# Two 64x64 projections as four array tiles, and a stage's loop written out

## The reference

```
left  = (a @ left_proj_w.T  + b) * sigmoid(a @ left_gate_w.T  + b)     (times a mask)
right = (a @ right_proj_w.T + b) * sigmoid(a @ right_gate_w.T + b)     (times a mask)
t     = einsum('bikc,bjkc->bijc', left, right)
t     = layernorm(t)
x2    = x + (t @ out_proj_w.T + out_proj_b) * sigmoid(a @ gating_w.T + gating_b)
p     = softmax(layernorm(x2) @ router_w + router_b)    over 8 experts
out   = x2 + sum over the 2 best experts of p_e / (p_1 + p_2) * (layernorm(x2) @ expert_w[e] + expert_b[e])
```

## Time and profile before

| what | us |
|---|---|
| median of three runs (lowest, highest) | 1189.2 (1185.09, 1192.96) |
| the profiled execution | 1189.99 |
| its span, first to last instruction | 1188.0 |
| PE busy in the span | 1080.7 |
| DVE | 882.2 |
| POOL | 747.6 |
| ACT | 598.8 |

### The profile page before, as it was taken

The page is one execution under the profiler, slowest core; times in us unless marked ns, Lnnn a source line. Parts: engine busy times, 40 slices in busy tenths (PEclk is TensorE's granted clock), DMA queues, the critical chain, the costliest instruction groups (busy, mean ns, idle before and its releaser), DMA issues.

```text
span 1188.0 us, 21300 instructions
## 1 busy us (share of the span) xinstructions
PE 1080.7 (91%) x5402; PEld 594.6 (50%) x5402; DVE 882.2 (74%) x3030; ACT 598.8 (50%) x1070; POOL 747.6 (63%) x728
## 2 busy tenths in 40 slices
PE   1788989889786599999999999999999999999987
PEld 1566666678674344444444444444444444454432
DVE  3999999611115768888888888887888788888872
ACT  0455666411111245666566556565656565656552
POOL 5777888121222357777777767776767776777632
PEclk9899999899887879999999999999999999999986
DMA  7388679967770101111111111111111111111100
GB/s 194 115 268 284 229 274 293 328 198 235 209 234 27 30 19 51 46 45 42 50 47 44 36 54 40 49 45 45 36 53 36 54 36 53 36 54 36 36 27 27
DMA packets 98895, 119.15 MB, mean 100 GB/s; under 512 B 6390, under 2 KB 72182, under 8 KB 96758
## 3 DMA queue, kind: packets, MB, share of 16 engines
q1 hardware_dynamic: 97138, 117.74, 30.9%
q10 hardware_dynamic: 1668, 0.46, 0.2%
HBM read 67.33 MB, written 50.33 MB: 99 GB/s over the span
## 4 chain that ended last, share of the span: by engine, by line
PE 75%; DVE 14%; issue 5%; DMA 2%; ACTq 1%; POOL 1%; ACT 1%; SPq 1%; DVEq 0%; POOLq 0%
PE b_m L807 22%; PE ring L793 9%; PE ein L710 7%; DVE stage L889 6%; PE b_d L754 6%; PE b_g L746 6%; PE b_t L747 5%; PE pr_a L672 4%; PE b_m L801 3%; DVE bst L876 3%; PE b_g L741 3%; PE b_g L735 3%; PE ring L815 3%; PE b_t L735 2%; PE ring L822 1%
## 5 line engine op out<-in xcount | busy, mean ns | idle before, releaser
L451 POOL TENSOR_TENSOR zb<-bcs,x2d 128x512 f32<-128x512 f32 x224 | 285.7, 1275 | 234.8 <-ACT bcs L588 233.6
L807 PE MATMUL b_m<-zb,w_exp 128*64 128x512 f32 x1024 | 284.7, 636 | 0.1
L1052 DVE TENSOR_TENSOR zb<-ring,x2d 128x512 f32<-128x512 f32 x288 | 197.5, 686 | 90.9 <-PE ring L793 90.2
L588 ACT ACTIVATE bcs<-ring 128x512 f32<-128x512 f32 x224 | 133.9, 598 | 245.5 <-PE ring L793 245.2
L572 ACT ACTIVATE x2d<-x2t 64x512 f32<-64x512 f32 x256 | 160.5, 627 | 3.4
L672 PE MATMUL pr_a<-w_proj,xts 64*128 64x256 f32 x1024 | 138.3, 399 | 22.1 <-DVE stage L889 21.4
L889 DVE SCALAR_TENSOR_TENSOR stage<-pr_a,mt,sig_a 128x128 f32<-128x128 f32 x512 | 147.8, 418 | 9.4 <-ACT sig_a L521 9.4
L793 PEld LDWEIGHTS ring<-wt,sel 32*128 32x128 f32 x512 | 49.4, 186 | 177.6 <-DVE zb L1052 83.1
L793 PE MATMUL ring<-wt,sel 32*128 32x512 f32 x512 | 131.0, 504 | 5.2 <-DVE zb L1052 4.4
L672 PEld LDWEIGHTS pr_a<-w_proj,xts 64*128 64x128 f32 x1024 | 95.1, 189 | 51.0 <-issue 30.9
L521 ACT ACTIVATE sig_a<-pr_a 128x512 f32<-128x512 f32 x128 | 76.4, 597 | 78.9 <-PE pr_a L672 78.9
(11 more groups left out here) (133 smaller groups left out, 1820.7 us busy)
## 6 DMA issues: line engine op xcount, KB each, us to landing
left_right_scratch<-stage SPq DMA_DIRECT2D x16, 2048.0 KB, 7.5
chunk<-left_right_scratch SPq DMA_DIRECT2D x24, 1024.0 KB, 9.0
xc<-in_x SPq DMA_DIRECT2D x64, 256.0 KB, 2.7
out<-outc SPq DMA_DIRECT2D x64, 256.0 KB, 2.0
chunk<-left_right_scratch SPq DMA_DIRECT2D x12, 384.0 KB, 7.5
chunk<-left_right_scratch SPq DMA_DIRECT2D x8, 192.0 KB, 4.9
chunk<-left_right_scratch SPq DMA_DIRECT2D x4, 256.0 KB, 8.0
chunk<-left_right_scratch SPq DMA_DIRECT2D x8, 64.0 KB, 4.7
```

The lines of the kernel that those rows point to most:

```text
L451: pool.tensor_tensor(zb[:, m % NZ, :], bcs[:, tiles_before(POOL_TILES, ku, ku, m) % 2, :], x2d[:, ku % 2, m % 2, :], ALU.mult)\
L588: act.activation(bcs[:, tiles_before(POOL_TILES, ku, ku, m) % 2, :], ring[:, bcast_bank(ku % 2, m), :], ACT.Copy).then_inc(bcast_out, 1)
L807: ins = pe.matmul(b_m[t * C:(t + 1) * C, :], w_exp[:, ep, :], zb[:, (2 * ep + t) % NZ, :], start=False, stop=ep == EP - 1, skip_group_chec ...
L1052: dve.tensor_tensor(zb[:, m % NZ, :], ring[:, bcast_bank(ku % 2, m), :], x2d[:, ku % 2, m % 2, :], ALU.mult)\
```

## The change

out_gate issues four matmuls of 64 rows by 64 columns. Tile (t, t) of the array, rows and columns of half t, multiplies the half t of xtn and writes the half t of b_g. Tile (t, 1 - t) multiplies the half t of ttn and writes the other half of b_t. So that each token's output lands in its own half, ScalarE's copy puts the upper half of b_t into the lower half of ttn and the other way round, in two copies of 64 partitions. The weights need no zeros: w_og is [128, 2, 64], and its memset goes. The semaphores g_ready and og_ready are raised by the last matmul of each kind.

The loops of all five engines in the last stage are written out: each slot is issued with its own number u, while ku, by which buffers are chosen, runs from 0 to 11 again and again.

```diff
-        w_og = keep("w_og", [P, 2, P])
+        w_og = keep("w_og", [P, 2, C])
...
-            pool.memset(w_og[:, :, :], 0.0).then_inc(pool_const, 1)
...
-                act.activation(ttn[:, :], b_t[:, :], ACT.Copy).then_inc(turns_out, 1)
+                for half in range(2):
+                    ins = act.activation(ttn[half * C:(half + 1) * C, :], b_t[(1 - half) * C:(2 - half) * C, :], ACT.Copy)
+                ins.then_inc(turns_out, 1)
...
             def out_gate(v):
                 pe.wait_ge(turns_out, v + 1)
-                pe.matmul(b_g[:, :], w_og[:, 0, :], xtn[:, :], start=True, stop=True).then_inc(g_ready, 1)
-                pe.matmul(b_t[:, :], w_og[:, 1, :], ttn[:, :], start=True, stop=True).then_inc(og_ready, 1)
+                half = [slice(t * C, t * C + C) for t in range(2)]
+                for t in range(2):
+                    g = pe.matmul(b_g[half[t], :], w_og[half[t], 0, :], xtn[half[t], :], start=True, stop=True)
+                    o = pe.matmul(b_t[half[1 - t], :], w_og[half[t], 1, :], ttn[half[t], :], start=True, stop=True)
+                g.then_inc(g_ready, 1)
+                o.then_inc(og_ready, 1)
...
-            for u in range(-4, 2 * HEAD):
-                slot(u, u)
-            with pe.Fori(0, LOOPS) as i:
-                for k in range(2 * HEAD, 2 * (HEAD + CYCLE)):
-                    slot(i * (2 * CYCLE) + k, k)
-            for u in range(2 * TAIL, UNITS + 1):
-                slot(u, u)
+            for u in range(-4, UNITS + 1):
+                slot(u, u % (2 * CYCLE) if u >= 0 else u)
...
-            dve.wait_ge(pool_const, 5)
+            dve.wait_ge(pool_const, 4)
...
-                    dve.tensor_copy(w_og[part, w, part], w_proj[part, (4 + w) * C:(5 + w) * C])
+                    dve.tensor_copy(w_og[part, w, :], w_proj[part, (4 + w) * C:(5 + w) * C])
```

More of the change, by code:

```diff
@@ L39 @@
 CYCLE = 6
-HEAD = 4
-LOOPS = (STEPS - 2 * HEAD) // CYCLE
-TAIL = HEAD + LOOPS * CYCLE
 TOK = STEP_J
@@ L313, in _ @@
                 load_unit(v, v)
-            for u in range(XC - 6, 2 * HEAD):
-                slot(u, u)
-            with sp.Fori(0, LOOPS) as i:
-                for k in range(2 * HEAD, 2 * (HEAD + CYCLE)):
-                    slot(i * (2 * CYCLE) + k, k)
-            for u in range(2 * TAIL, UNITS + 1):
-                slot(u, u)
+            for u in range(XC - 6, UNITS + 1):
+                slot(u, u % (2 * CYCLE) if u >= 0 else u)
             for h in range(2):
@@ L482, in _ @@
             ins.then_inc(sel_made, 1)
[L483 to L489, removed]
+            for u in range(-3, UNITS):
+                slot(u, u % (2 * CYCLE) if u >= 0 else u)
         @block.scalar
```

## The result

The changed kernel takes 1149.4 us (median of three runs, 1146.6 to 1158.81) where the one before takes 1189.2: a ratio of 0.9685, with a 95% interval of 0.9642 to 0.9727. A second set of runs gave 1146.42 against 1190.38: 0.9641 (0.9613 to 0.967). The forecast was 1151.5, in a range of 1138 to 1178. Ratios are of the mean times of the fast executions; the one slow execution, 1191.6 us of the loop alone, is left out, and since that kernel's profile is of it, only its full pipe, at clock 1.00, is compared.

A forecast was written before the change was run, and what follows sets the result against it. The prediction took PE (TensorE) to bound the last stage. From the profiled 1190.0 us it took 7.1 for the loop and 32.2 for the projections and added 0.8 for the fill: 1151.5 us, range 1138 to 1178.

The forecast's parts named there:

- The loop, 7.1 us: Last stage: three jumps back, each with the slot behind it costing 2.36 us, vanish when written out; 7.1 us saved.
- out_gate and the turns, 2.36 to 1.60: PE's projections and following turns: four tiles overlap in 1.01 us, turns take 0.59; 0.76 us saved a slot.
- The odd slot keeps 0.33, the even one 0.76: Full pipe: ScalarE's gate sigmoid limits odd slots' saving to 0.33 us; even slots keep all 0.76; 32.2 us over 59 units.
- PE's share of the stage was to fall to about 95%: Last stage: PE's busy share down from 99% to about 95%, a sign expected in the profile after.
- ScalarE's copy, 0.5 to 0.63 us later, covered except in the fill: ScalarE's added ttn copy raises turns_out 0.5 to 0.63 us later, delaying PE only in the fill's four units.
- The fill, +0.8: Fill: four units each pay 0.5 us for the copy and win back about 0.3; 0.8 us added.
- The drain, 0: Work left after the last unit's out_gate starts: the forecast sum gave it no term.
- What came before the stage, 0: Very start of the kernel: w_og's memset goes where PE is not the bound; 0 us.
- partial overlap: Rival on out_gate: passes start in staggered pairs, 1164.2 us, or ScalarE's run slips, 1169; chance 0.18.
- two groups one behind the other: Rival on out_gate: g and g, o and o cannot run together; 1190 us, no change; chance 0.08.
- rival 3: out_gate's passes start in program order, four tiles taking 2.30 us; slower, 1215 us; chance 0.05.
- Fetching the long code: Rival on the written-out loops: code fetching stops engines as the jump did, 7.1 us stay; 1158.6 us; chance 0.11.

The follow-up runs named there:

- e1: The kernel before with its five engines' loops written out, projections as before; 1187.14 us against 1192.25, ratio 0.9945.

## Why the prediction was right

Step by step, by the full pipe's 58 periods:

- *The loop, 7.1 us.* 7.0 in the first profile of before, 8.4 in the second, where the clock fell at a jump. Right, with two small terms that were put at nothing and nearly cancel: 0.5 for entering the loop, and 0.6 for the even slots, a little longer when written out. That no stop comes back: right (PE busy 682.50 of 682.50).
- *out_gate and the turns, 2.36 to 1.60.* The four tiles and the turns behind took 1.02 + 0.59 = 1.61 in even slots, and 0.75 was saved wherever nothing else was late. Right, and taken from the two nearest rows.
- *The odd slot keeps 0.33, the even one 0.76.* Measured 11.97 - 11.63 = 0.34 and 11.56 - 10.82 = 0.74. The cause named, ScalarE's sigmoid behind its run of copies, is shown by moving it. That tile 6 stands right behind it was in the prediction too, and is shown by the version that moves both. Of the 0.4 us that PE was to wait for the sigmoid at x_turn, it waits 0.17 at the turns for tile 6 and 0.23 at x_turn for the sigmoid. PE's share of the stage was to fall to about 95%, and is 98.8% (643.14 of 651.00): waits of 0.4 us in 29 slots are 1.8% of the stage, so that number didn't follow from the prediction's own. Both steps together: e1's 682.4 less 651.1 is 31.3 us, against 32.2 for 59 units.
- *ScalarE's copy, 0.5 to 0.63 us later, covered except in the fill.* Covered in the full pipe, yes: without it the periods are the same. Its size was under-read: ttn is done 1.81 us after xtn's start (1046.63 to 1048.44), where it was 1.08 before (1103.37 to 1104.45 in an odd slot), so 0.73. ttn's two halves start 0.61 us apart (1047.24 and 1047.85), where a copy of 128 partitions starts 0.49 behind the one ahead of it.
- *The fill, +0.8.* Measured 56.9 against 59.2. The sign is wrong, and the number is the difference of larger ones: the second and third unit took 9.64 us each instead of 6.86, the fourth and fifth 15.95 and 10.72 instead of 21.41 and 13.11.
- *The drain, 0.* Measured -7.9 and -5.5 us against the two profiles of before. This term was missing. The drain's length goes with the time that TensorE spends at the half level in it (29.0 and 24.6 us before, 8.6 after), as the last section shows; what sets that time is open.
- *What came before the stage, 0.* The first out_gate started at 386.9 us, against 381.7 and 384.5 before: 5.2 and 2.4 later. Of the 5.2, 0.7 is the second copy, as above. The rest lies ahead of the stage: the einsum's last pass ended at 373.6 us, against 369.2 and 371.9 before, two profiles of one kernel that are 2.7 apart, and 370.7 in the version without the swap, which has no memset either.

So the forecast of 1151.5 is right in its large terms, 39.3 foreseen and 38.3 measured for the full pipe. The profiled execution, 1146.6, is 4.9 below it: 1.0 less saved in the pipe and 5.2 more in front, against 3.1 less in the fill and 7.9 less in the drain. That the median came out within some 2 us of the forecast is luck: these terms cancel in part, and the median of the three lies 2.8 above the profiled one.

Of the rivals: partial overlap, and two groups one behind the other, fall with the eight starts above; the second is exactly what the version without the swap does (2.46 us, 1187). Program order, as rival 3 had it, falls with the same starts: out_gate takes 1.02 us and not 2.30. The trace has no order of the instructions other than their starts, so whether the passes also stand in the stream in that order is not shown, for these tiles as for L807's halves; the prediction's word that the trace disagrees there was too strong. Fetching the long code falls with the loop alone. The rule of the Trainium skill (TensorEngine Tiling (Array Packing), Restrictions and Gotchas) that different row tiles cannot access one PSUM bank at the same time did not show: the two L731 passes of different rows write b_g together, at 1050.07 and 1050.08, in different partitions. Whether it holds for the same partitions of one bank was not tried. The four at once, and the piece of 1.02 us, agree with the span model in the Trainium skill, TensorE: Matmul & The Clock Gate, packing small matmuls (The mechanism), by which each further tile adds about 4 ns to one matmul: here some 7 ns from one start to the next.

## What to carry to other kernels

Two small projections of two halves fill the array if each half's second product is sent to the other column half: the swap costs one more copy ahead, and without it there is no gain at all. Before counting a saving on the engine that bounds, find for each kind of iteration the next engine's last operation and its slack: that gave 0.33 and 0.76 instead of twice 0.76, and named the two operations whose moving brought the rest (11 us more). Fit the comparison to the stretch that was changed: here whole times carry differences of up to 11 us from a drain whose work was the same.

## What the runs showed of the hardware that I had not expected

Drains with the same work differ by 11 us, and go with the time that TensorE spends in them at its half level: 46.6 us with 0.9 at the half level (both moved, clock 0.99), 46.8 with 1.2 (the sigmoid early), 48.8 with 5.0 (eight pieces), 49.8 and 49.8 with 8.6 and 8.5 (changed kernel, 0.91), 55.0 and 55.0 with 24.7 (one copy, 0.78), 55.5 with 24.8 (without the swap), 57.7 with 29.5 (the projections alone), and 55.3 with 24.6 and 57.7 with 29.0 (the two profiles of before, 0.78 and 0.75). That is 0.4 us of drain for 1 us at the half level. PE's busy time in them goes from 35.5 to 47.4 us, while the other engines stay within 0.4 us from profile to profile.

Two profiles of one kernel agree to 0.1 us in fill and drain for the changed kernel and for the one with one copy; the drains of before do not (57.7 and 55.3). Nor does the agreement reach the other executions: the kernel with one copy took 1147.7 us at a mean clock of 0.956 and 1155.4 at 0.948, the changed kernel 1145.7 at 0.960 and 1158.8 at 0.945. So the clock of these stretches can't be called a property of the kernel, and that an edit moved it is not shown.

In the fill, the second unit's x_turn, four transposes, takes 1.11 us in the changed kernel and 0.65 before:

```profile
399.70 1.11 PE L724 MATMUL b_g<-turn_route,xc 128*128 128x128 f32 x4 [0.70 <-ACT sig_c L550]
```

The granted clock of 399.7 to 400.8 us is 0.50, the half level (1.2 GHz). It comes after 0.70 us of idle time and an out_gate of about 1.1 us, where before it followed an out_gate of 1.8 us with no pause. What decides which stretches are granted the full clock is not settled by these runs. A jump of the hardware loop cost 13.98 - 11.97 = 2.0 us each of the three times in the first profile. In the two other profiles with jumps it cost 1.9 to 3.3: 3.3, 1.9 and 2.2 in the kernel before, 2.2, 3.3 and 3.3 with the projections alone; the three that cost 3.3 are those behind whose stop the clock fell to its half level (1.2 GHz).
